# Attention layer, 16 images on one core: the first image's preparation reordered, the output weight summed in place and split during the first scores

## The chip, the cores and the metric

The kernel runs on one core of a Trainium2 chip. The metric is the device time of one execution in microseconds (us), and the median of several runs is compared. Engines are named as in the profile: PE is TensorE's matmul, PEld its weight load, DVE VectorE, ACT ScalarE, POOL GpSimd, SP SyncE, which issues most of the transfers.

## The reference, cut to what matters

```python
# x: (16, 512, 32, 32) float32, the weights are 512 x 512
h = group_norm(x, gamma, beta)          # 32 groups, eps 1e-6
q, k, v = conv1x1(h, wq, bq), conv1x1(h, wk, bk), conv1x1(h, wv, bv)
attn = einsum('bci,bcj->bij', qf, kf) * 512 ** -0.5
attn = softmax(attn, axis=2)
out = einsum('bcj,bij->bci', vf, attn)
return x + conv1x1(out, wo, bo)
```

## The kernel before

Each image is a matrix h of 512 channels by 1024 positions. The kernel folds the weights: the scores need only the product of wk and wq (called `wkq`), and the output needs only the product of wv and wo (`wov`), with the biases folded in as `t_bias` (from wk and bq) and `out_bias` (from wo, bv and bo). Both products are formed once. Every fp32 product is made of three matmuls, high by high, high by low and low by high, where "high" is a copy rounded by ACT (a CAST row) and "low" is what DVE subtracts to get the rest. A call of `product` is therefore three matmuls, on lines 315, 316 and 317.

**Preparation, once.** SP loads wo, wv, wk, wq and the first image. PE transposes wo (L326), which needs `ident` from POOL (L268). ACT and DVE split the transposed wo, POOL subtracts for wv (L272). PE forms `wov` (48 matmuls), then `wkq` (48 matmuls), and in between the bias sums (L346, L350, L352): matmuls of one column. `wov` is copied to SBUF, split, and stored in DRAM (`kept_v`). Then `wkq` is copied to SBUF, four differences are made of it (L809 to L814), and seven blocks are split into `w_split` (L543 on ACT, `wt_high`; L799 and L803 on DVE, `wt_split`), which SP stores as `kept_t`. The statistics of the first image come from `bn_piece` and `group_variance`; `normalise` (L527) applies them, `sum_h` (L737 to L745) makes four sums of the blocks, and `high_h` and `low_h` (L536, L752) split seven blocks.

**Each image.** `make_t` forms T in two halves r of seven products p (order `T_ORDER`), each six matmuls. `make_scores` forms 28 products of six matmuls in the order `S_ORDER`: four of p=7, then two pairs of q with p = 1, 6, 5, 3, 2, 4. ACT takes a snapshot of the bank after some products (L640, `s_snapped`), and the next product into that bank waits for it. DVE adds (L913, `add_s`), keeps the running maximum (L922, `max_step`), and takes the statistics of the next image from 8 pieces (L684), which SP loads. `make_v` forms 8 products of twelve matmuls; from the fifth on, j=4, it needs `v_split` (L938) to free a bank. `outputs_0` and `outputs_1` follow, 96 products. SP reloads `w_split` twice per image: from `kept_v` when T is done, from `kept_t` when V is done. The order on each engine is written out by hand, with semaphores between engines; an engine waits in order, so whatever stands behind a waiting instruction waits too.

Of the kernel before, what the change touches and what calls it, by code (L numbers as in the profile page):

```python
# [5 lines left out]
F32 = mybir.dt.float32  # L6
# [7 lines left out]
P = 128  # L14
# [17 lines left out]
T_AT = {p: n + 1 for n, p in enumerate(T_ORDER)}  # L32

# [20 lines left out]
def attention_program(nc, x, gamma, beta, wq, bq, wk, wv, bv, wo, bo, out):  # L54
# [15 lines left out]
    bq_d, *vec_d = [a.rearrange("(k p) -> p k", p=P) for a in (bq, gamma, beta, bo, bv)]  # L70
# [5 lines left out]
    with ExitStack() as ctx:  # L76
# [20 lines left out]
        bq_s, vecs = sb("bq_s", [KC]), sb("vecs", [4, KC])  # L97
        gamma_s, beta_s, bo_s, bv_s = (vecs[:, n, :] for n in range(4))
        t_bias, out_bias, t_step = sb("t_bias", [KC]), sb("out_bias", [KC]), sb("t_step", [2])
# [12 lines left out]
        for n, b_ in enumerate((S1, S3, S2, S4)):  # L112
            blocks[b_] = scores[:, 2 * n:2 * n + 2, :]

# [15 lines left out]
        wq_hi, wq_lo, wk_hi, wk_lo = big_hi[:, 0:4, :], big_lo[:, 0:4, :], big_hi[:, 4:8, :], big_lo[:, 4:8, :]  # L130
        wvs_hi, wvs_lo, wot_hi, wot_lo = big_hi[:, 8:12, :], big_lo[:, 8:12, :], big_hi[:, 12:16, :], big_lo[:, 12:16, :]
        wkq, wd_t, wov = scores[:, 0:4, :], scores[:, 4:8, :], scores[:, 12:16, :]
        first_v_hi, first_v_lo = (a[:, NJ:NJ + 6, :].rearrange("p (b k) n -> p b k n", k=2) for a in (big_hi, big_lo))
# [12 lines left out]
        bank = [ctx.enter_context(nc.psum_tensor(f"bank{n}", [P, 512], F32)) for n in range(8)]  # L146
# [4 lines left out]
        def o_bank(n):  # L151
            return bank[n]

        bq_in, vec_in = sem("bq_in"), sem("vec_in")
# [20 lines left out]
        wk_high, wq_high, wv_high, wot_high, wkq_copied, wov_copied, wt_high, wvs_high = (  # L175
            sem(n) for n in ("wk_high", "wq_high", "wv_high", "wot_high", "wkq_copied", "wov_copied", "wt_high",
# [7 lines left out]
        biases_set = sem("biases_set")  # L184
# [20 lines left out]
        def _(sp):  # L205
            for o in range(KC):
                sp.dma_start(wo_raw[:, o, :], w_d["o"][:, o, :]).then_inc(wo_in[o], 16)
            for o in range(KC):
                sp.dma_start(wv_raw[:, o, :], w_d["v"][:, o, :]).then_inc(wv_in[o], 16)
            for o in range(KC):  # L210
                sp.dma_start(wk_raw[:, o, :], w_d["k"][:, o, :]).then_inc(wk_in[o], 16)
                sp.dma_start(wq_raw[:, o, :], w_d["q"][:, o, :]).then_inc(wq_in[o], 16)
            for k in range(KC):
                sp.dma_start(full[:, k, :], x_d[0][:, k, :]).then_inc(x0_in[k], 16)

            sp.wait_ge(wvs_split, 3)
            sp.dma_start(kept_v[:, 0, :], big_hi[:, NJ:NJ + 6, :].rearrange("p a n -> p (a n)").bitcast(F32)).then_inc(kept_v_out, 16)
            sp.dma_start(kept_v[:, 1, :], big_lo[:, NJ:NJ + 6, :].rearrange("p a n -> p (a n)").bitcast(F32)).then_inc(kept_v_out, 16)
            sp.wait_ge(wt_split, 7)
            sp.dma_start(kept_t, w_split[:].bitcast(F32)).then_inc(kept_t_out, 16)  # L220
            sp.wait_ge(kept_v_out, 32)
            sp.wait_ge(kept_t_out, 16)

            def image(b, more):
# [8 lines left out]
                if more:  # L233
# [8 lines left out]
                sp.wait_ge(t_summed, count(b, 14, 14))  # L242
                sp.dma_start(w_split[:, :, 0:VW].bitcast(F32), kept_v).then_inc(wvs_in, 16)
                if more:
# [9 lines left out]
                    sp.wait_ge(v_summed, count(b, 8, 8))  # L254
                    sp.dma_start(w_split[:].bitcast(F32), kept_t).then_inc(wt_in, 16)


            images(sp, image)
# [4 lines left out]
        def _(pool):  # L263
            nc.gpsimd.memset(ident[:], 0.0).then_inc(consts_set, 1)
            nc.gpsimd.memset(minus_half[:], -0.5).then_inc(consts_set, 1)
            nc.gpsimd.memset(primer[:], 0.0).then_inc(consts_set, 1)
# [3 lines left out]
            for o in range(KC):  # L270
# [11 lines left out]

            deviation(0)
            prime()
# [28 lines left out]
        def _(pe):  # L313
# [8 lines left out]
            pe.wait_ge(consts_set, 4)  # L322
            for c in range(KC):
                pe.wait_ge(wo_in[c], 16)
                for n in range(KC):
                    mm = nc.tensor.transpose(bank[KC + n][:, cols(c)], wo_raw[:, c, cols(n)], ident[:])  # L326
                    if c == KC - 1:
                        mm.then_inc(wo_turned, 1)

            for o in range(KC):  # L330
                pe.wait_ge(wot_split, o + 1)
                pe.wait_ge(wv_split, o + 1)
                for c in range(KC):
                    mm = product(bank[c][:], wvs_hi[:, o, cols(c)], wvs_lo[:, o, cols(c)],
                                 wot_hi[:, o, :], wot_lo[:, o, :], o == 0, o == KC - 1)
                    if o == KC - 1:
                        mm.then_inc(wov_summed, 1)

            def bias_sums():

                pe.wait_ge(bq_in, 16)
                pe.wait_ge(vec_in, 16 * len(vec_d))
                pe.wait_ge(wov_copied, 1)
                for c in range(KC):
                    for o in range(KC):
                        nc.tensor.matmul(bank[0][:, c:c + 1], wk_raw[:, o, cols(c)], bq_s[:, o:o + 1],  # L346
                                         start=o == 0, stop=o == KC - 1, skip_group_check=True)
                for c in range(KC):
                    for o in range(KC):
                        nc.tensor.matmul(bank[0][:, KC + c:KC + c + 1], wot_hi[:, o, cols(c)].bitcast(F32),  # L350
                                         bv_s[:, o:o + 1], start=o == 0, stop=False, skip_group_check=True)
                        mm = nc.tensor.matmul(bank[0][:, KC + c:KC + c + 1], wot_lo[:, o, cols(c)].bitcast(F32),  # L352
                                              bv_s[:, o:o + 1], start=False, stop=o == KC - 1, skip_group_check=True)
                mm.then_inc(bias_summed, 1)

            for o in range(KC):
                pe.wait_ge(wk_split, o + 1)
                pe.wait_ge(wq_split, o + 1)
                for c in range(KC):
                    mm = product(bank[KC + c][:], wq_hi[:, o, cols(c)], wq_lo[:, o, cols(c)],  # L360
# [3 lines left out]
                if o == KC - 2:  # L364
                    bias_sums()
# [9 lines left out]
            def make_t(b):  # L375
                for r in range(2):
                    for p in T_ORDER:
                        if r == 0:
                            pe.wait_ge(h_split, count(b, 7, H_AT[OF_H[p]]))

                            pe.wait_ge(wt_split, T_AT[p])

                        if p == 4:
                            pe.wait_ge(o_scaled, count(b, 8, (1, 4)[r]))
                        if p == 7:
                            pe.wait_ge(o_scaled, count(b, 8, (2, 5)[r]))
                        if p == 5:
                            pe.wait_ge(o_scaled, count(b, 8, (3, 6)[r]))
# [675 lines left out]
```

## Time and profile before

| | us |
|---|---|
| median of 3 runs | 2062.42 (2057.86 to 2062.47) |
| profiled execution, its own time | 2057.07 |
| its span, first to last instruction | 2055.4 |
| PE busy | 2014.2 (98% of the span) |
| DVE busy | 1619.7 (79%) |
| ACT busy | 955.4 (46%) |

The difference between the profiled execution's time and its span is 1.7 us. A wait of PE lengthens the run directly, since PE is busy for nearly all of it outside the beginning.

### The profile page before, as it was taken

To read this page: it belongs to the slowest core of one execution; us is meant where nothing else is said; L and a number is where in the kernel's file an instruction comes from. 1 tells how busy PE (TensorE), PEld (TensorE's weight loads), DVE (VectorE), ACT (ScalarE), POOL (GpSimd) and SP (SyncE) were. 2 spreads that over 40 slices of the span, in tenths; PEclk is the share of its full clock that TensorE was granted. 3 is DMA by queue.
4 is the path that set the end of the run, shared out by engine and by line. 5 is a ranking of instruction groups with operands and counts; after the bars stand their busy time and mean duration, and the time that the engine had idled before them with its cause. 6 is when DMAs were issued, how large, how long until landed. Compare 5 with 4: busy or idle time off the path is not lost.

```text
span 2055.4 us, 26986 instructions
## 1 busy us (share of the span) xinstructions
PE 2014.2 (98%) x8848; PEld 1661.7 (81%) x8848; DVE 1619.7 (79%) x2112; ACT 955.4 (46%) x1427; POOL 325.2 (16%) x236
## 2 busy tenths in 40 slices
PE   7699999999999999999999999999999999999998
PEld 6488888888888888888888888888888888888886
DVE  3769697787978879697787978879697787968866
ACT  2635463452635445463453635445364443645442
POOL 1002012120201202012120202202011120201202
PEclk8799999999999999999999999999999999999999
DMA  3524335252343424335252343424335242343402
GB/s 123 222 96 143 113 153 143 85 139 108 125 135 153 101 83 146 109 153 143 86 138 112 122 133 153 106 77 150 105 153 143 98 127 112 127 128 153 93 10 41
DMA packets 57124, 248.79 MB, mean 121 GB/s; under 512 B 8208, under 2 KB 8208, under 8 KB 50192
## 3 DMA queue, kind: packets, MB, share of 16 engines
q1 hardware_dynamic: 36032, 214.97, 27.4%
q0 software_dynamic: 18432, 33.56, 10.9%
q10 hardware_dynamic: 2640, 0.01, 0.1%
q8 instruction: 10, 0.16, 0.0%
q14 instruction: 10, 0.08, 0.0%
HBM read 208.15 MB, written 73.92 MB: 137 GB/s over the span
## 4 chain that ended last, share of the span: by engine, by line
PE 91%; DMA 4%; DVE 2%; issue 1%; ACT 1%; POOL 0%; DVEq 0%; POOLq 0%; ACTq 0%
PE bank L315 30%; PE bank L317 30%; PE bank L316 30%; DMA out<-scores 4%; ACT scores L607 1%; DVE scores L835 0%; DVE h_lo L752 0%; DVE wide L954 0%; PE bank L352 0%; PE bank L350 0%; ACT room L527 0%; PE bank L346 0%; POOL out L307 0%; DVE w_split L803 0%; PE bank L326 0%
## 5 line engine op out<-in xcount | busy, mean ns | idle before, releaser
L315 PE MATMUL bank<-big_hi 128*128 128x512 f32 x1056 | 412.0, 390 | 0.8 <-DVE big_lo L760 0.8
L316 PE MATMUL bank<-big_lo,big_hi 128*128 128x512 f32 x1056 | 411.7, 390 | 0.0
L317 PE MATMUL bank<-big_hi,big_lo 128*128 128x512 f32 x1056 | 411.6, 390 | 0.0
L315 PE MATMUL bank<-big_hi,h_hi 128*128 128x512 f32 x896 | 349.8, 390 | 0.6
L317 PE MATMUL bank<-big_hi,h_lo 128*128 128x512 f32 x896 | 348.7, 389 | 0.0
L316 PE MATMUL bank<-big_lo,h_hi 128*128 128x512 f32 x896 | 348.7, 389 | 0.0
L913 DVE TENSOR_TENSOR scores<-bank,room 128x512 f32<-128x512 f32 x192 | 131.0, 689 | 194.2 <-ACT room L640 141.3
L640 ACT COPY room<-bank 128x512 f32<-128x512 f32 x192 | 112.8, 587 | 278.6 <-PE bank L317 278.6
L315 PEld LDWEIGHTS bank<-big_hi 128*128 128x128 f32 x1056 | 198.8, 188 | 42.6 <-DVE big_lo L760 1.2
L316 PEld LDWEIGHTS bank<-big_lo,big_hi 128*128 128x128 f32 x1056 | 198.8, 188 | 41.3
L317 PEld LDWEIGHTS bank<-big_hi,big_lo 128*128 128x128 f32 x1056 | 198.8, 188 | 41.2
L290 POOL PARTITION_ALL_REDUCE wide<-red x32 | 56.9, 1828 | 922.6 <-DVE red L922 922.6
L315 PEld LDWEIGHTS bank<-big_hi,h_hi 128*128 128x128 f32 x896 | 168.2, 188 | 40.1 <-issue 5.4
L315 PE MATMUL bank<-w_split,h_hi 128*128 128x512 f32 x512 | 199.2, 389 | 0.0
L316 PE MATMUL bank<-w_split,h_hi 128*128 128x512 f32 x512 | 199.2, 389 | 0.0
L317 PE MATMUL bank<-w_split,h_lo 128*128 128x512 f32 x512 | 199.2, 389 | 0.0
L315 PE MATMUL bank<-h_hi,w_split 128*128 128x512 f32 x448 | 177.5, 396 | 21.0 <-DVE w_split L803 8.3
L316 PEld LDWEIGHTS bank<-big_lo,h_hi 128*128 128x128 f32 x896 | 168.2, 188 | 34.8
L317 PEld LDWEIGHTS bank<-big_hi,h_lo 128*128 128x128 f32 x896 | 168.2, 188 | 34.8
L601 ACT CAST big_hi<-scores 128x512 fp32r<-128x512 f32 x256 | 147.8, 618 | 77.0 <-PE bank L317 75.0
L587 ACT CAST big_hi<-bank 128x512 fp32r<-128x512 f32 x128 | 75.2, 587 | 223.6 <-PE bank L317 223.5
L301 POOL PARTITION_ALL_REDUCE wide<-red x32 | 117.7, 3677 | 371.0 <-DVE red L950 357.1
(104 smaller groups left out, 3301.9 us busy)
## 6 DMA issues: line engine op xcount, KB each, us to landing
w_split<-kept_t SPq DMA_DIRECT2D x15, 3584.0 KB, 11.1
w_split<-kept_v SPq DMA_DIRECT2D x16, 3072.0 KB, 10.5
out<-scores POOLq DMA_DIRECT2D x128, 256.0 KB, 7.1
room<-in_x SPq DMA_DIRECT2D x30, 1024.0 KB, 5.9
room<-in_x SPq DMA_DIRECT2D x60, 256.0 KB, 3.6
red<-in_x SPq DMA_DIRECT2D x30, 256.0 KB, 3.4
wide<-in_x SPq DMA_DIRECT2D x30, 256.0 KB, 7.2
kept_t<-w_split SPq DMA_DIRECT2D x1, 3584.0 KB, 9.9
```

The lines of the kernel that those rows point to most:

```text
L290: nc.gpsimd.partition_all_reduce(wide[:, half, :], red[:, half, :], P, MAX_ALL).then_inc(max_all, 1)
L301: nc.gpsimd.partition_all_reduce(wide[:, half, :], red[:, half, :], P, ADD_ALL).then_inc(sum_all, 1)
L315: nc.tensor.matmul(o, a_hi, b_hi, start=start, stop=False, skip_group_check=True)
L316: nc.tensor.matmul(o, a_hi, b_lo, start=False, stop=False, skip_group_check=True)
L317: return nc.tensor.matmul(o, a_lo, b_hi, start=False, stop=stop, skip_group_check=True)
L587: nc.scalar.copy(v_hi[:, j, :], bank[v_ring[j % 4]][:]).then_inc(v_high, 1)
L601: nc.scalar.copy(p_hi[:, j, :], scores[:, half * NJ + j, :]).then_inc(p_high, 1)
L607: nc.scalar.activation(scaled(n), scaled(n), ACT.Identity, bias=out_bias[:, c:c + 1]).then_inc(o_done, 1)
L640: nc.scalar.copy(snap_s(q, n), bank[alpha_s[q % 2]][:]).then_inc(s_snapped, 1)
L913: nc.vector.tensor_tensor(scores[:, o, :], bank[at][:], snap_s(q, n), ALU.add).then_inc(s_added, 1)
```

## The change

It touches only the beginning and the first image; from the second image on the instructions are the same. SP now loads wk and wq first, then the first image (in the order of blocks 2, 3, 0, 1), then wv and wo. PE forms `wkq` first, into banks 0 to 3, then the rest of the bias sum of wk and bq, then the 16 transposes of wo, then `wov` into banks 4 to 7. The bias sum of wo and bv leaves PE: DVE makes it in the first scores with four multiply-and-reduce instructions (`tensor_tensor_reduce`), from wo and bv loaded again. `wkq` is no longer copied to SBUF, except one block (`b12_copy`). The copies of `wov`, its split and its store to `kept_v` move from the preparation into the first image: copies during T, the split on ACT (`high_wv`) and DVE (`first_weights`) during the first scores, written straight into `w_split`, so that the first V needs no reload. The first image's blocks are split partly inside its T. The pieces of the second image are loaded after `wvs_split`, and six of the eight are worked on at the end of the first pair of scores, the other two in the second pair. PE and SP have the first image written out ahead of their loop.

```diff
         def _(sp):
             for o in range(KC):
-                sp.dma_start(wo_raw[:, o, :], w_d["o"][:, o, :]).then_inc(wo_in[o], 16)
+                sp.dma_start(wk_raw[:, o, :], w_d["k"][:, o, :]).then_inc(wk_in[o], 16)
+                sp.dma_start(wq_raw[:, o, :], w_d["q"][:, o, :]).then_inc(wq_in[o], 16)
+            for k in (2, 3, 0, 1):
+                sp.dma_start(full[:, k, :], x_d[0][:, k, :]).then_inc(x0_in[k], 16)
             for o in range(KC):
                 sp.dma_start(wv_raw[:, o, :], w_d["v"][:, o, :]).then_inc(wv_in[o], 16)
...
+                if first:
+
+                    sp.wait_ge(t_split, 14)
+                    for c in range(KC):
+                        sp.dma_start(wo_again[c], w_d["o"][:, c, :]).then_inc(wo_back, 16)
+                    sp.dma_start(bv_rows, bv.partition_broadcast(P)).then_inc(bv_in, 16)
+                    sp.wait_ge(wvs_split, 3)
+                    for n in range(6):
+                        piece(n)
+                    sp.dma_start(kept_v, w_split[:, :, 0:VW].bitcast(F32)).then_inc(kept_v_out, 16)
...
+            bias_sum(0)
             for o in range(KC):
                 pe.wait_ge(wk_split, o + 1)
                 pe.wait_ge(wq_split, o + 1)
                 for c in range(KC):
-                    mm = product(bank[KC + c][:], wq_hi[:, o, cols(c)], wq_lo[:, o, cols(c)],
+                    mm = product(bank[c], wq_hi[:, o, cols(c)], wq_lo[:, o, cols(c)],
                                  wk_hi[:, o, :], wk_lo[:, o, :], o == 0, o == KC - 1)
...
+            for o in range(1, KC):
+                bias_sum(o)
+            pe.wait_ge(consts_set, 4)
+            for c in range(KC):
+                pe.wait_ge(wo_in[c], 16)
+
+            pe.wait_ge(t_bias_set, 1)
+            for n in range(KC):
+                for c in range(KC):
+                    mm = nc.tensor.transpose(bank[KC + n][:, cols(c)], wo_raw[:, c, cols(n)], ident[:])
+                mm.then_inc(wo_turned, 1)
+            pe.wait_ge(wot_split, KC)
...
+            act.wait_ge(wd_set, 4)
+            for p in W_ORDER:
+                high_wt(p)
+            for k in (2, 3):
                 normalise(0, k)
-            high_h(0, 0)
...
+            def high_wv(n):
+
+                act.wait_ge(t_summed, 14)
+                act.wait_ge(kept_t_out, 16)
+                if n == 2:
+                    act.wait_ge(wdv_set, 1)
+                else:
+                    act.wait_ge(wov_copied, KC)
+                nc.scalar.copy(wv_hi[:, n, :, :], wov_step if n == 2 else wov[n]).then_inc(wvs_high, 1)
...
                         nc.scalar.copy(scores[:, NJ + q, :], bank[alpha_s[q % 2]][:]).then_inc(c12_copied, 1)
+                    if first and pair == 0:
+                        high_wv(2)
...
+            def first_weights():
+
+
+                dve.wait_ge(t_split, 14)
+                dve.wait_ge(wov_copied, KC)
+                nc.vector.tensor_tensor(wov_step, wov[1], wov[0], ALU.subtract).then_inc(wdv_set, 1)
+                dve.wait_ge(wdv_set, 1)
+                for n in range(3):
+                    dve.wait_ge(wvs_high, n + 1)
+                    nc.vector.tensor_tensor(wv_lo[:, n, :, :], wov_step if n == 2 else wov[n],
+                                            wv_hi[:, n, :, :].bitcast(F32), ALU.subtract).then_inc(wvs_split, 1)
+                dve.wait_ge(wo_back, 16 * KC)
+                dve.wait_ge(bv_in, 16)
+                for c in range(KC):
+                    if c:
+                        dve.wait_ge(bv_used, c)
+                    nc.vector.tensor_tensor_reduce(out=wo_bv_terms, in0=wo_again[c], in1=bv_rows, scale=1.0,
+                                                   scalar=0.0, op0=ALU.mult, op1=ALU.add,
+                                                   accum_out=wo_bv[:, c:c + 1]).then_inc(bv_used, 1)
...
+                    if first and pair == 0:
+                        first_weights()
+                        for n in range(6):
+                            next_piece(b, n)
```

The order on SP's queue at the start, first before and then after (wk, wq, wo, wv are `in_wk` and so on, `room<-in_x` is the first image).

```order
L207 DMA scores<-in_wo 128x512 x4
L209 DMA scores<-in_wv 128x512 x4
L211 DMA scores<-in_wk 128x512
L212 DMA scores<-in_wq 128x512
L211 DMA scores<-in_wk 128x512
```

```order
L219 DMA scores<-in_wk 128x512
L220 DMA scores<-in_wq 128x512
L222 DMA room<-in_x 128x1024 x4
L224 DMA scores<-in_wv 128x512 x4
L226 DMA scores<-in_wo 128x512 x4
L229 DMA kept_t<-w_split 128x7168
```

The pair wk, wq stands four times on each side; it moved from the ninth place to the first, and the image moved ahead of wv and wo.

The order on ACT at the end of the first T and in the first scores (L640 and L696 are the snapshots, L644 and L703 the last copy of a pair, L606 is `high_wv`), before and then after.

```order
L583 CAST big_hi<-scores 128x512 x3
L640 COPY room<-bank 128x512 x6
L644 COPY scores<-bank 128x512 x2
L640 COPY room<-bank 128x512 x6
L644 COPY scores<-bank 128x512 x2
```

```order
L622 CAST big_hi<-scores 128x512 x3
L606 CAST w_split<-wide 128x1024
L606 CAST w_split<-room 128x1024
L696 COPY room<-psum 128x512 x6
L703 COPY scores<-psum 128x512 x2
L606 CAST w_split<-scores 128x1024
L696 COPY room<-psum 128x512 x6
L703 COPY scores<-psum 128x512 x2
```

The third cast of `high_wv` now stands between the copies of the first pair and the snapshots of the second.

The order on DVE in the first scores (L913 and L972 add, L922 and L981 take the maximum, L684 and L747 the statistics of a piece), before and then after.

```order
L684 BN_STATS bn<-wide 128x6 x2
L913 TENSOR_TENSOR scores<-bank,room 128x512 x2
L684 BN_STATS bn<-room 128x6 x2
L913 TENSOR_TENSOR scores<-bank,room 128x512 x2
L922 TENSOR_TENSOR red<-scores 128x1024
L913 TENSOR_TENSOR scores<-bank,room 128x512 x2
L922 TENSOR_TENSOR red<-red,scores 128x1024 x2
L913 TENSOR_TENSOR scores<-bank,room 128x512 x2
L696 BN_AGGR chan<-bn 128x2 x4
```

```order
L981 TENSOR_TENSOR red<-red,scores 128x1024 x2
L1026 TENSOR_TENSOR scores<-room,wide 128x1024
L1030 TENSOR_TENSOR w_split<-wide,w_split 128x1024
L1030 TENSOR_TENSOR w_split<-room,w_split 128x1024
L1030 TENSOR_TENSOR w_split<-scores,w_split 128x1024
L1037 ISA scores,wo_bv<-scores 128x512
L1037 ISA wo_bv 128x1
L1042 TENSOR_TENSOR out_bias<-wo_bv,vecs 128x4
L747 BN_STATS bn<-room 128x6 x2
L747 BN_STATS bn<-wide 128x6 x2
L972 TENSOR_TENSOR scores<-psum,room 128x512 x2
L747 BN_STATS bn<-room 128x6 x2
```

The two L1037 rows stand four times each. The work of `first_weights` and the six pieces now stands between the maxima of the first pair and the additions of the second, and the last two pieces stand ahead of the statistics' end (L759 after, L696 before).

## Rows read from the trace of the kernel before

**Rows 1.** The page: the span, and the busy time of each engine.
```profile
span 2055.4 us, 26986 instructions
PE 2014.2 (98%) x8848; PEld 1661.7 (81%) x8848; DVE 1619.7 (79%) x2112; ACT 955.4 (46%) x1427; POOL 325.2 (16%) x236
```

**Rows 2.** Windows, PE alone: width, PE busy, PE's granted clock, DMA share, GB/s.
```profile
0.00:4.00 4.00, 0.00 (x0) 1.00 0.36 69
0.00:8.00 8.00, 0.00 (x0) 1.00 0.72 190
0.00:16.00 16.00, 4.03 (x18) 1.00 0.90 282
0.00:20.00 20.00, 8.03 (x35) 1.00 0.93 307
...
84.00:98.00 14.00, 14.00 (x63) 1.00 0.34 114
```

**Rows 3.** Timeline of the start: start, us, engine, line, operation, tiles, idle before.
```profile
8.71 0.62 ACT L511 CAST big_hi<-scores 128x512 fp32r<-128x512 f32 x1 [6.06 <-DMA scores<-in_wv]
11.21 3.67 PE L326 MATMUL bank<-ident,scores 128*128 128x128 f32 x16 [11.21 <-POOL ident L268]
15.46 3.80 POOL L272 TENSOR_TENSOR big_lo<-scores,big_hi 128x512 fp32r<-128x512 f32 x3 [3.05 <-ACT big_hi L511]
23.95 4.83 DVE L684 BATCH_NORM_STATS2 bn<-room 128x6 f32<-128x512 f32 x8
31.61 0.16 DVE L722 SCALAR_TENSOR_TENSOR var_g<-square_g,chan_g 128x4 f32<-128x4 f32 x1
```

**Rows 4.** Windows, PE alone, where its granted clock falls and rises.
```profile
36.00:38.00 2.00, 2.00 (x20) 1.00 0.00 0
38.00:40.00 2.00, 2.00 (x17) 0.79 0.00 0
40.00:42.00 2.00, 2.00 (x11) 0.50 0.00 0
...
58.00:62.00 4.00, 0.00 (x0) 0.70 1.05 442
...
80.00:82.00 2.00, 1.38 (x3) 0.50 1.25 426
```

**Rows 5.** Timeline, 34 to 81 us, of PE, ACT and DVE.
```profile
34.83 3.63 PE L346 MATMUL bank<-bq_s,scores 128*128 128x1 f32 x32
51.44 1.99 ACT L550 CAST big_hi<-scores 128x1024 fp32r<-128x1024 f32 x2 [23.99 <-PE bank L352]
57.04 4.63 ACT L527 ACTIVATE room<-room,h_shift,h_scale 128x1024 f32<-128x1024 f32 x4
62.66 3.74 ACT L543 ACTIVATE w_split<-scores 128x512 fp32r<-128x512 f32 x7
65.73 2.49 DVE L803 TENSOR_TENSOR w_split<-scores,w_split 128x512 fp32r<-128x512 f32 x4
75.20 2.35 DVE L752 TENSOR_TENSOR h_lo<-scores,h_hi 128x1024 fp32r<-128x1024 f32 x2
80.62 0.79 PE L315 MATMUL bank<-h_hi,w_split 128*128 128x512 f32 x1 [3.43 <-ACT scores L574]
```

**Rows 6.** Timeline, the first scores and V, of PE, ACT and DVE.
```profile
98.46 0.39 PE L315 MATMUL bank<-big_hi,h_hi 128*128 128x512 f32 x1
121.14 2.49 DVE L922 TENSOR_TENSOR red<-red,scores 128x1024 f32<-128x1024 f32 x2
121.78 0.59 ACT L640 COPY room<-bank 128x512 f32<-128x512 f32 x1 [6.21 <-PE bank L317]
127.94 0.69 DVE L913 TENSOR_TENSOR scores<-bank,room 128x512 f32<-128x512 f32 x1 [4.31 <-ACT room L640]
138.52 2.48 DVE L922 TENSOR_TENSOR red<-red,scores 128x1024 f32<-128x1024 f32 x2
```

**Rows 7.** DMA issues: KB each, us from issue to landing.
```profile
kept_v<-big_lo SPq DMA_DIRECT2D x1, 1536.0 KB, 9.6
```

More of the change, by code:

```diff
@@ L210, in _, with image @@
             for o in range(KC):
[L211 to L218, printed above, removed]
+                sp.dma_start(wo_raw[:, o, :], w_d["o"][:, o, :]).then_inc(wo_in[o], 16)
             sp.wait_ge(wt_split, 7)
             sp.dma_start(kept_t, w_split[:].bitcast(F32)).then_inc(kept_t_out, 16)
-            sp.wait_ge(kept_v_out, 32)
-            sp.wait_ge(kept_t_out, 16)
-            def image(b, more):
+            def image(b, more, first=False):
                 sp.dma_start(out_d[b], x_d[b].rearrange("p k n -> k p n")).then_inc(rest_in, 16)
@@ L231, in piece @@
                                  x_d[b + 1][:, k, half * HALF:(half + 1) * HALF]).then_inc(piece_in[n % 6], 16)
-                if more:
+                if more and not first:
                     sp.wait_ge(h_split, count(b, 7, 7))
@@ L254, in image @@
                     sp.wait_ge(v_summed, count(b, 8, 8))
+                    if first:
+                        sp.wait_ge(kept_v_out, 16)
                     sp.dma_start(w_split[:].bitcast(F32), kept_t).then_inc(wt_in, 16)
-            images(sp, image)
+            image(0, True, True)
+            with sp.Fori(1, B - 1) as b:
+                image(b, True)
+            image(B - 1, False)
             for n in range(2 * KC):
@@ L499, in image @@
                     pe.wait_ge(wt_in, count(b, 16, 16))
-            images(pe, image)
+            image(0, True, True)
+            with pe.Fori(1, B - 1) as b:
+                image(b, True)
+            image(B - 1, False)
         @block.scalar
@@ L610, in image @@
             def image(b, more, first=False):
-                act.wait_ge(h_split, count(b, 7, 7))
+                if not first:
+                    act.wait_ge(h_split, count(b, 7, 7))
+                else:
+                    act.wait_ge(bias_summed, 1)
                 for r in range(2):
@@ L615, in image @@
                         snap(b, r, 0, "a", T_AT[4])
-                        if not first:
+                        if first:
+                            copy_wov(0)
+                            copy_wov(1)
+                        else:
                             for n in (KC, KC + 1):
@@ L624, in image @@
                     snap(b, r, 2, "y", T_AT[6])
+                    if r == 0 and first:
+                        high_h(0, 6, True)
                     high_t(b, r, "D1")
@@ L632, in image @@
                     high_t(b, r, "B21")
+                    if r == 0 and first:
+                        copy_wov(2)
+                        copy_wov(3)
+                if first:
+                    for n in range(2):
+                        high_wv(n)
                 for pair in range(2):
@@ L966, in image @@
                     q0, q1 = 2 * pair, 2 * pair + 1
-                    if more and pair == 0:
+                    if more and pair == 0 and not first:
                         for n in range(6):
                             next_piece(b, n)
-                    if more and pair == 1:
+                    if more and pair == 1 and not first:
                         dve.wait_ge(bn_set, count(b + 1, PIECES, PIECES))
@@ L973, in image @@
                     add_s(b, "C22", q1)
-                    if more and pair == 0:
+                    if more and pair == (1 if first else 0):
                         for n in range(6, 8):
                             next_piece(b, n)
+                    if first and pair == 1:
+                        dve.wait_ge(bn_set, count(b + 1, PIECES, PIECES))
                     if more and pair == 1:
```

288 lines of the change are left out of this document (147 added, 141 removed).

## The prediction

> **What bounds the kernel now.** The page first: PE is busy for 2014.2 of 2055.4 us [rows 1], so 41 us of idle are all that can be won by filling gaps; the other possible gain is PE work that is removed or that ran slowly. Then the windows of PE with its granted clock. From 84 to 98 us PE is busy throughout at clock 1.00 [rows 2], as it is in all later images. The beginning is different: PE starts at 11.21 us [rows 3], its clock falls to 0.50 between 38 and 42 us and stands there at 80 us [rows 4], and the first score matmul comes at 98.46 [rows 6]. Fourteen products of six matmuls lie ahead of it in T, and at full clock a product takes 1.36 us, a matmul 0.227: ACT begins the snapshot of the 17th score product at 121.78 [rows 6], and (121.6 - 98.46) / 17 is 1.36. So T alone is worth 84 x 0.227 = 19.1 us, and some 79 us of 98.5 are preparation.
>
> The timeline says where they go. 32 rows of one-column matmuls take 3.63 us at full clock [rows 5], and 64 more such rows, with the clock fallen, reach to 51.4, when ACT ends a wait of 23.99 us for them. Then ACT and DVE work nearly alone up to 80.62, where PE begins to run without a break [rows 5].
>
> **The start.** I take the loading from the mean rates: 0.28 MB in 4 us, 1.52 MB in 8, 4.51 in 16 and 6.14 in 20 [rows 2]. ACT saw the fifth transfer (1.31 MB in all, moved at about 7.4) at 8.71 [rows 3], so a transfer is seen 1.3 us after its last byte. In the new order: the first wk and wq are seen at 5.2 and 6.2, the fourth pair at 11.0, the image at 16.6, wv at 17.2 to 19.2, wo at 21.2 or so. A cast (0.62) and a subtraction (0.7) after 6.2 let PE begin on `wkq` at 7.7, instead of on transposes at 11.21.
>
> At what clock? The windows show 1.00 from the start [rows 2], but PE did nothing in them. When PE came back from a pause at 80.62 it was at 0.50 for 3 us [rows 4, 5], and I go by that: about 4.8 us at half clock, 11 of 48 matmuls, the rest at 0.227: 4.8 + 8.4 after 7.7 gives 21.0. The other bound is full clock at once, 2 us less. [...]
>
> **From `wkq` to T.** The remaining bias sum is 12 matmuls in 24 rows at 3.63/32: 2.7 us, to 23.7. ACT copies `t_bias` (0.3), then 16 transposes take 3.67 [rows 3], to 27.7. ACT and DVE split the last of four, 0.6 and 0.7, with DVE free: its statistics end 3.0 us after the last piece, as 31.77 stands to 28.78 [rows 3], thus 20.9, and four differences take 2.7 more. POOL's subtractions for wv, 3.80 for three [rows 3], now run from 22.0 to 25.8 behind the power for the statistics; in time. `wov` begins at 29.2. Its 48 matmuls take 10.9 at full clock, to 40.1.
>
> Here the clock matters once more. One-column matmuls and waits fill 21.0 to 24.0, and PE waits again after 27.7. Before, 4 us of such matmuls brought the clock down [rows 4, 5], and 3 us of pause did (0.70 in 58 to 62 [rows 4]). I take it to fall, which costs half of some 4.8 us: 2.4, so `wov` ends at 42.5. Bounds: 0 and 3.5.
>
> The other engines over the same time: ACT 3.74 for the high parts of `w_split` (28.4 to 32.2), 4.63 for normalising and 1.04 for the first block [rows 5], to 37.8; DVE's four of the seven low parts take 2.49, so 4.3 for seven, done by 34.4. Then sums and splits of 1.2 each [rows 5] on DVE: block 2 of seven at 41.4, 3 at 42.5, 4 at 43.7. These are ready when T wants them. The remaining three are not: ACT casts block 5 only after the snapshot of the third product, and DVE's queue holds sum and split of 1.2 each. The first half of T, 9.5 us of matmuls, takes 13.2 in my list (gaps of 1.7 ahead of the fifth and 1.9 ahead of the seventh product). The second half takes 9.6. T ends at 42.5 + 13.2 + 9.6 = 65.3, against 98.46: 33.2 us less.
>
> **What the first image gets instead.** I keep to the clock of the trace before; everything in it comes 33.2 earlier. `first_weights` waits for the maxima of the first pair, which end at 121.14 + 2.49 = 123.6 [rows 6]. The difference (1.2) ends at 124.9, and only then can ACT do the third cast of `high_wv` (1.04), to 126.0. Behind it on ACT stand the snapshots of the second pair; the first, at 121.78 before [rows 6], is now at 126.0 to 126.6. PE has (1, q=2) and (1, q=3) done at 123.1, and its next product waits for that snapshot: 3.5 us of new wait.
>
> DVE: three low parts, 1.2 each, to 128.4; four multiply-and-reduce with an accumulator read each, which no row shows. The nearest rows are 0.69 for 128x512 [rows 6] and 1.24 for twice the size; I take 0.95 with the read, 3.8 in all (bounds 2.8 and 6). Then six pieces, 4.83/8 each [rows 3], 3.6, which are loaded from 128.4 on. Total to 136.0. The next addition, at 127.94 before [rows 6], ends at 136.7. PE wants it for (4, q=2), at 134.0 before, now 137.5: just covered. Pieces 7 and 8 queue behind the store of `kept_v`, 3 MB, which took 9.6 us before [rows 7]; they are seen at about 141.5, and DVE waits for them ahead of all else. Then 1.2 for them, 3.0 of statistics, and 7.8 for four additions of 0.69 and four maxima of 1.24, with small gaps: the maxima end at 153.5 instead of 138.52 + 2.48 = 141.0 [rows 6]. The first `low_v` ends at 154.2. PE wants it for the fifth product of V, 38.1 + 10.9 us after 98.46, plus the 3.5: 151.0. That is 3.2 of wait. If the pieces came in time (138.3), `low_v` would be at 149.7 and the wait nothing.
>
> After that DVE is 9.9 late and PE 6.7; low parts of the second half are wanted at the very time that they are ready, so I add nothing. One return from half clock after these pauses costs about 1.6 (half of the 3.2 after 80.6 [rows 4]). Together: 3.5 + 3.2 + 1.6 = 8.3.
>
> **Sum.** -33.2 + 8.3 = -24.9, from the profiled execution's 2057.07: 2032. The three runs before lie 0.8 to 5.4 above that execution, so the median of after may lie above it too; I add 1 and say 2033.
>
> **Rivals.**
> A. The forecast: T some 33 us earlier, 5 to 11 given back. 2027 to 2037. Chance 0.55.
> B. The new waits are covered: the pieces land early, the clock stays up between `wkq` and `wov`. Gain 33.2 + 2.4 less 3.5 and a margin of 1: 31, 2026 and down to 2021. For it: DMA is mostly free there; against it: ACT's wait of 3.5 comes from order alone. Chance 0.17.
> C. More is lost in the first image: multiply-and-reduce at the upper bound (+2.2), and the lateness of DVE carries through the second half and into the next T (3 to 6), or the preparation's splits on ACT and DVE take 5 us longer. 2037 to 2050. DVE is busy 79% [rows 1], so such a delay ends within an image or two. Chance 0.21.
> D. The other side: PE stays at half clock. If the many short waits of the first T and scores kept the clock at 0.50 throughout, each matmul would take 0.43 instead of 0.227: over T, scores and V of the first image (84 + 168 + 96 matmuls) 348 x 0.2 = 70 us lost against 25 won. It decides from some 50 us at half clock, 120 matmuls or so over the 25 us. Against it: the clock came back within 4 us of unbroken work at 80.62 to 84 [rows 2, 4], and the gaps here are single ones between stretches of 5 to 20 us. Chance 0.03, with 0.04 for a net gain too small to be told (within 0.3%, 6 us, about what a measurement of this kernel can tell).
>
> **How the numbers follow.** A and B and C up to 2045 hold over 0.8: the range is 2022 to 2045. Faster by more than 0.3% (below 2056) holds A, B and C: 0.93; same 0.04; slower 0.03.
>
> **What would show it.** First score matmul at 65 (60 to 69) instead of 98.46. PE's first product near 7.7 and first at half clock. `wov` from 29 to 42. Two idle gaps of 1.5 to 2 us in the first half of T. A PE wait of about 3.5 us for ACT's snapshot some 25 us after the first score, and one of about 3 for `low_v` some 52 us after it. Later images unchanged. I would be wrong if the chain of waits showed ACT or DVE behind the block splits for longer, if transposes wait for wo, or if the written-out first image made PE wait for instructions.

## The result and the profile after

| | before | after |
|---|---|---|
| median of the runs, us | 2062.44 (2057.86 to 2063.1, 4) | 2036.33 (2035.51 to 2037.96, 4) |
| profiled execution, us | 2057.07 | 2037.96 |
| span, us | 2055.4 | 2036.3 |

The ratio is 0.988, 95% interval 0.9864 to 0.9896: faster by 1.2%. Forecast were 2033 us and the range 2022 to 2045. The medians are 26.1 us apart and the two profiled executions 19.1, because the median of before lies 5.4 above its profiled execution and that of after 1.6 below its own. All accounts below are of profiled executions.

The page of the kernel after, its first two rows, against [rows 1].

```profile
span 2036.3 us, 26714 instructions
PE 2005.2 (98%) x8784; PEld 1652.2 (81%) x8784; DVE 1624.8 (80%) x2119; ACT 954.0 (47%) x1425; POOL 325.5 (16%) x236
```

PE's share is 98% in both, so the page tells nothing of where 19 us went. Landmarks do: the first score matmul, and the reloads of `w_split`, which SP issues when V and T are done. The first score stood at 98.46 before [rows 6]. The two reloads of before, then the timeline rows of after:

```profile
158.49 0.35 SPq L255 DMA_DIRECT2D w_split<-kept_t  x1
...
221.05 0.58 SPq L243 DMA_DIRECT2D w_split<-kept_v  x1
```

```profile
6.95 0.76 PE L340 MATMUL psum<-big_hi 128*128 128x512 f32 x1 [0.43 <-DVE big_lo L827]
20.00 2.73 PE L352 MATMUL psum<-bq_s,scores 128*128 128x1 f32 x24
23.07 1.94 PE L375 MATMUL psum<-ident,scores 128*128 128x128 f32 x16 [0.34 <-ACT t_bias L575]
27.64 0.50 PE L340 MATMUL psum<-big_hi 128*128 128x512 f32 x1 [2.63 <-DVE big_lo L852]
63.04 0.39 PE L340 MATMUL psum<-big_hi,h_hi 128*128 128x512 f32 x1
...
135.52 0.34 SPq L275 DMA_DIRECT2D w_split<-kept_t  x1
...
201.95 0.62 SPq L261 DMA_DIRECT2D w_split<-kept_v  x1
```

So the lead over the kernel before is 98.46 - 63.04 = 35.4 us at the first score, 23.0 at the end of the first V, 19.1 at the end of the second image's T, and still 19.1 at the end. More was won in the preparation than the net shows, and 16.3 us were given back within the next 140 us.

Where it was given back is in the list of PE's waits up to 170 us (total, times, longest), of which these are three lines.

```profile
PE psum L340 <- ACT room L696: 3.5, 1, 3.5
PE psum L340 <- DVE big_lo L997: 3.2, 1, 3.2
PE psum L340 <- DVE h_lo L816: 3.1, 2, 1.6
```

The first two are the two waits of the forecast; the third is the two gaps in T. From 170 to 204 us one more, in the second image's T, where before there was none:

```profile
PE psum L340 <- DVE scores L885: 2.3, 1, 2.3
```

The timeline shows the chain behind the first two. DVE's difference of the output weight (L1026) releases ACT's cast (L606), behind which the snapshots stand; then DVE waits 6.62 us for the last two pieces, and the low part of v is that much later.

```profile
88.13 1.22 DVE L1026 TENSOR_TENSOR scores<-room,wide 128x1024 f32<-128x1024 f32 x1
89.46 1.04 ACT L606 CAST w_split<-scores 128x1024 fp32r<-128x1024 f32 x1 [9.31 <-DVE scores L1026]
90.41 1.07 ACT L696 COPY room<-psum 128x512 f32<-128x512 f32 x2
91.14 0.76 PE L340 MATMUL psum<-big_hi,h_hi 128*128 128x512 f32 x1 [3.45 <-ACT room L696]
109.28 1.33 DVE L747 BATCH_NORM_STATS2 bn<-room 128x6 f32<-128x512 f32 x2 [6.62 <-DMA room<-in_x]
121.68 0.79 PE L340 MATMUL psum<-w_split,h_hi 128*128 128x512 f32 x1 [3.23 <-DVE big_lo L997]
```

And windows of PE with its granted clock (columns as in [rows 2]) show what follows each pause.

```profile
80.00:90.00 10.00, 7.68 (x34) 0.99 0.00 0
90.00:95.00 5.00, 3.87 (x9) 0.50 0.19 66
95.00:100.00 5.00, 5.00 (x20) 0.84 0.93 274
120.00:125.00 5.00, 3.32 (x8) 0.55 0.93 372
125.00:130.00 5.00, 5.00 (x19) 0.76 0.11 39
```

A mean of 0.84 over 5 us is 1.6 us at 0.50; with the 5 us before and 0.2 at the end of the window of 0.99 that is 6.8 us at half clock, of which PE paused 1.3: 5.5 us of work that took twice its time, 2.7 us lost. The second spell is 4.5 + 2.4 us, less 1.2 of pause: 2.9 lost. The third, after the wait in the second image, is 3.4 us long (0.72 over 198 to 204): 1.7 lost. The account closes: 3.5 + 3.2 + 2.7 + 2.9 = 12.3 of the 12.4 us up to the end of V, and 2.3 + 1.7 = 4.0 of the 3.9 after it. ("Half clock" is 0.50 in the column: the matmuls from 92 to 96 us start 0.43 us apart, those around them 0.23.)

### The profile page after: what moved, and what is told of

The parts are those of the page before. It is cut to its first block, busy times and chain, and to the rows that moved or that the text cites. A ratio compares the mean times of both kernels' runs of the same rounds, so it can differ in the third digit from the quotient of the medians.

```text
span 2036.3 us, 26714 instructions
## 1 busy us (share of the span) xinstructions
PE 2005.2 (98%) x8784; PEld 1652.2 (81%) x8784; DVE 1624.8 (80%) x2119; ACT 954.0 (47%) x1425; POOL 325.5 (16%) x236
## 4 chain that ended last, share of the span: by engine, by line
PE 86%; DMA 5%; DVE 1%; issue 1%; ACT 1%; POOL 0%; DVEq 0%; POOLq 0%; ACTq 0%
PE psum L340 29%; PE psum L342 28%; PE psum L341 28%; DMA out<-scores 5%; ACT scores L646 1%; DVE scores L885 0%; DVE wide L1013 0%; DVE red L981 0%; POOL out L332 0%; DVE scores L1019 0%; DVE scores L1005 0%; DVE scores L972 0%; DVE scores L1007 0%; POOLq L79 0%; DVE big_lo L992 0%
## 5 line engine op out<-in xcount | busy, mean ns | idle before, releaser
L340 PE MATMUL psum<-big_hi 128*128 128x512 f32 x1056 | 413.2, 391 | 3.1 <-DVE big_lo L852 2.6
L341 PE MATMUL psum<-big_lo,big_hi 128*128 128x512 f32 x1056 | 412.6, 391 | 0.0
L342 PE MATMUL psum<-big_hi,big_lo 128*128 128x512 f32 x1056 | 412.6, 391 | 0.0
L340 PE MATMUL psum<-big_hi,h_hi 128*128 128x512 f32 x896 | 351.5, 392 | 4.0 <-ACT room L696 3.5
L341 PE MATMUL psum<-big_lo,h_hi 128*128 128x512 f32 x896 | 350.1, 391 | 0.0
L342 PE MATMUL psum<-big_hi,h_lo 128*128 128x512 f32 x896 | 350.0, 391 | 0.0
L972 DVE TENSOR_TENSOR scores<-psum,room 128x512 f32<-128x512 f32 x192 | 130.9, 689 | 195.2 <-ACT room L696 141.8
L696 ACT COPY room<-psum 128x512 f32<-128x512 f32 x192 | 112.7, 587 | 274.6 <-PE psum L342 274.6
L340 PEld LDWEIGHTS psum<-big_hi 128*128 128x128 f32 x1056 | 199.1, 189 | 44.5 <-DVE big_lo L852 2.9
L341 PEld LDWEIGHTS psum<-big_lo,big_hi 128*128 128x128 f32 x1056 | 199.3, 189 | 41.6
L340 PE MATMUL psum<-w_split,h_hi 128*128 128x512 f32 x512 | 200.7, 392 | 3.2 <-DVE big_lo L997 3.2
L342 PE MATMUL psum<-w_split,h_lo 128*128 128x512 f32 x512 | 200.4, 391 | 0.0
L341 PE MATMUL psum<-w_split,h_hi 128*128 128x512 f32 x512 | 200.4, 391 | 0.0
L640 ACT CAST big_hi<-scores 128x512 fp32r<-128x512 f32 x256 | 147.8, 619 | 75.2 <-PE psum L342 73.2
```

The source lines that it names most:

```text
L340: nc.tensor.matmul(o, a_hi, b_hi, start=start, stop=False, skip_group_check=True)
L341: nc.tensor.matmul(o, a_hi, b_lo, start=False, stop=False, skip_group_check=True)
L342: return nc.tensor.matmul(o, a_lo, b_hi, start=False, stop=stop, skip_group_check=True)
L640: nc.scalar.copy(p_hi[:, j, :], scores[:, half * NJ + j, :]).then_inc(p_high, 1)
L696: nc.scalar.copy(snap_s(q, n), bank[alpha_s[q % 2]][:]).then_inc(s_snapped, 1)
L972: nc.vector.tensor_tensor(scores[:, o, :], bank[at][:], snap_s(q, n), ALU.add).then_inc(s_added, 1)
```

## The experiments

All are timed against the kernel before on the same chip; "after" stands for the changed kernel. The landmark "first score" is the start of the first score matmul in each trace.

**The changed kernel again.**

> The changed kernel once more, to have it beside the next three. All theories: 2036 us (2035 to 2038), first scores begin some 35 us earlier than before, V of the first image ends some 23 us earlier, and PE waits 3.5 us for ACT's snapshot and 3.2 us for DVE's low part of v. If the 2.3 us wait of PE in the second image's T is an accident of the transfers, it differs here; if the new order makes it, it is here again.

Measured: 2037.58 us (2034.25 to 2040.85), ratio 0.9898 (0.9872 to 0.9924), 21.9 below the median of before in the same measurement. First score at 63.06, waits of 3.5 and 4.0, and 2.1 us in the second image's T. By the same windows the three spells at half clock cost some 1.7, 2.4 and 1.7 here, against 2.7, 2.9 and 1.7 in the first trace: the first wait is 3.5 us long in both, and what came behind it is not the same. The wait in the second image's T is made by the new order, not an accident: it also came in the next three kernels (1.2, 1.2, 2.2).

**The output weight's difference taken earlier on DVE (e1).**

```diff
                     q0, q1 = 2 * pair, 2 * pair + 1
...
+                    if first and pair == 0:
+                        dve.wait_ge(t_split, 14)
+                        dve.wait_ge(wov_copied, KC)
+                        nc.vector.tensor_tensor(wov_step, wov[1], wov[0], ALU.subtract).then_inc(wdv_set, 1)
                     add_s(b, "C22", q0)
```

> The difference of the output weight is taken on DVE ahead of the first scores' additions, where DVE stood idle for 8 us, so ACT's third cast no longer waits and the snapshots behind it are in time. Theory 1 (two waits in series on one DVE chain: the second one is set by DVE and by the late pieces): PE's 3.5 us wait for the snapshot goes, but DVE's chain is only 1.2 us shorter, so PE then waits some 8 us instead of 3.2 for the low part of v; the time falls by 1 to 2 us only, to 2035. Rival (the waits add up, each can be taken away by itself): 3.5 us and the half-clock spell after it, 2.8 us, are won, 2030.

Measured: 2035.29 us (2034.0 to 2036.98). PE's waits from 60 to 170 us:

```profile
PE psum L340 <- DVE big_lo L997: 3.3, 1, 3.3
PE psum L340 <- DVE scores L972: 3.2, 1, 3.2
```

The wait for ACT is gone and the time is the same within the noise, as theory 1 says; the rival's 2030 falls. The place was not quite as expected: part of the wait came back at the first addition of the second pair (L972), which DVE gives only after the six pieces. It was "just covered" in the forecast, and is the next wait in the line.

**The store behind the pieces (e2).**

```diff
                     for n in range(6):
                         piece(n)
-                    sp.dma_start(kept_v, w_split[:, :, 0:VW].bitcast(F32)).then_inc(kept_v_out, 16)
...
                         piece(n)
+                    if first:
+                        sp.dma_start(kept_v, w_split[:, :, 0:VW].bitcast(F32)).then_inc(kept_v_out, 16)
```

> The 3 MB store of the split output weight is issued behind the loads of the last two pieces instead of ahead of them. Theory 1 (the last two pieces stand behind the store, DVE waited 6.6 us for them, and PE in turn 3.2 us for DVE): DVE's wait for the pieces goes from 6.6 to under 1 us, PE's 3.2 us wait for v's low part and the half-clock spell after it (2.8 us) go, 6 us in all, 2030; the wait for the snapshot (3.5) stays. Rival (the pieces are late because they are issued late, whatever is ahead of them): DVE still waits 3 us or more, and the time stays within 1 us of 2036.

Measured: 2029.48 us (2026.95 to 2030.69). DVE's wait for the pieces in `room` fell from 6.6 to 0.4 us, and one wait of PE is left between 60 and 170 us:

```profile
PE psum L341 <- ACT room L697: 3.4, 1, 3.4
```

Theory 1 holds: the two pieces were late because 3 MB of store stood ahead of them in the queue. In after that store took 13.0 us to land:

```profile
kept_v<-w_split SPq DMA_DIRECT2D x1, 3072.0 KB, 13.0
```

The 9.6 us of [rows 7], with which the forecast reckoned, are for half as much, 1536 KB. It was the second of two such stores, issued at 56.31 and 56.68, so both together had landed 10.0 us after the first was issued.

**Both (e12).**

> Both edits. Theory 1: the snapshot is in time, the pieces are in time; DVE gives v's low part at about 113.8 us of the run and PE wants it at 112.1, so a wait of 1 to 2 us is left and no half-clock spell or a short one: 10 to 11 us less, 2026. Rival of e1 (waits simply add): 12.4 us less, 2024. Rival of e2: no more than e1 alone gives.

Measured: 2029.39 us (2028.13 to 2031.05), 3 us above theory 1 and no better than the store alone. PE's wait at L973, the first addition of the second pair, is 3.1 us long: with the snapshot in time PE simply arrives there sooner. The 1.7 us expected at the low part of v were put at the wrong place; DVE's six pieces and bias sum between the pairs are the limit. Part of the gain was also lost again behind it: the first V ended at 128.30 instead of 131.05 with the store alone, but PE's wait in the second image's T was 2.2 us long with a spell at half clock behind it (0.50 in 192 to 194 us), instead of 1.2 without one (1.00 from 190 to 204), and the second image's T ended at 194.60 against 195.07.

**The whole split in DVE's idle time (e4).**

```diff
+                    if first and pair == 0:
+                        first_weights()
                     add_s(b, "C22", q0)
                     add_s(b, "C22", q1)
+                    if first and pair == 0:
+                        for n in range(6):
+                            next_piece(b, n)
...
                     if first and pair == 0:
-                        first_weights()
-                        for n in range(6):
-                            next_piece(b, n)
+                        first_bias()
```

`first_bias` is the last part of `first_weights`, the sum with bv; ACT's third cast goes ahead of the first snapshot.

> The whole split of the output weight is done ahead of the first scores' additions, where DVE stood idle for 8 us (ACT's three casts ahead of the first snapshot), the six pieces are loaded and worked on in the first pair, and only the bias sum stays at its end. Theory 1 (all of what was given back comes from DVE's queue at the turn of the pairs and the spells at half clock behind its waits): no PE wait over 0.5 us in the first scores and V, no half-clock spell there, V of the first image ends at 123 to 124 us instead of 135.5, and DVE is not late in the second image; the time falls by 12 to 16 us, 2020 to 2025. Rival 1 (the same work on DVE moves the waits elsewhere: first snapshot, or the maxima): V ends at 127 or later, 2028 or more. Rival 2 (PE's wait of 1.2 to 2.3 us in the second image's T is one of the output stores, not of DVE's lateness): it stays here.

Measured: 2022.18 us (2020.96 to 2024.37), ratio to before 0.9828 (0.981 to 0.9847). From 60 to 170 us there is no PE wait in the list at all, and the clock is full throughout:

```profile
60.00:140.00 80.00, 80.00 (x354) 1.00 0.49 181
```

The first V ends at 123.4 instead of 135.5. Both rivals fall; the wait in the second image is gone too, so it was DVE's lateness that made it. How late DVE was shows at its last four output products of the first image, behind which its last stores come. Before and in after:

```profile
202.15 2.48 DVE L960 TENSOR_TENSOR scores<-bank,wide 128x512 f32<-128x512 f32 x4
180.75 2.48 DVE L1019 TENSOR_TENSOR scores<-psum,wide 128x512 f32<-128x512 f32 x4
```

That is 43.7 us behind the end of V before and 45.2 in after; here it is 43.7 again (167.09). In the traces where it is 44.7 to 46.3, PE waits 0.7 to 2.3 us at this place, and where it is 43.7, not at all or 0.6 (e7 below). DVE's own wait for the stores was there before, 2.5 us, is 5.6 in after and 3.4 here.

DVE's rows show where the work went: into the time in which it stood idle for 8.0 us in after.

```profile
68.42 1.23 DVE L1024 TENSOR_TENSOR scores<-room,wide 128x1024 f32<-128x1024 f32 x1
69.68 1.23 DVE L1028 TENSOR_TENSOR w_split<-wide,w_split 128x1024 fp32r<-128x1024 f32 x1
70.83 1.22 DVE L1028 TENSOR_TENSOR w_split<-room,w_split 128x1024 fp32r<-128x1024 f32 x1
71.96 1.22 DVE L1028 TENSOR_TENSOR w_split<-scores,w_split 128x1024 fp32r<-128x1024 f32 x1
76.52 0.69 DVE L970 TENSOR_TENSOR scores<-psum,room 128x512 f32<-128x512 f32 x1 [3.35 <-ACT room L696]
```

**Scale and shift behind the subtractions that PE waits for (e6).** `affine(0)` moves behind the loop over `wot_lo` on DVE.

> As e4_split_first, and the three small instructions of the first image's scale and shift are put behind the four subtractions for the transposed weight. In the changed kernel two of the three took 0.91 and 1.20 us instead of 0.15 while POOL subtracted for wv. Theory: they are lengthened by POOL's instructions, and stand ahead of what PE waits for; the output weight's product begins 1.2 us sooner, and the time is 1 to 1.5 us under e4. Rival: the subtractions themselves are lengthened by POOL in their place, and nothing is won.

Measured: 2018.16 us (2017.7 to 2021.58), ratio 0.981 (0.9791 to 0.983). First score 61.96, against 63.26 in the kernel without this edit, 1.3 us sooner, as expected. The median is 4.0 lower, more than the 1 to 1.5 of the theory, and the rest is not shown to come from the edit: T of the second image ends 1.3 us sooner (184.99 against 186.30), T of the sixth at the same time (678.06 against 678.07), though the instructions in between are the same. The rows of DVE in after, and then in this one:

```profile
22.85 0.91 DVE L790 TENSOR_TENSOR h_scale<-vecs,rstd 128x4 f32<-128x4 f32 x1
23.79 1.20 DVE L792 TENSOR_TENSOR mean_scaled<-chan_g,h_scale 128x4 f32<-128x4 f32 x1
25.11 2.48 DVE L852 TENSOR_TENSOR big_lo<-psum,big_hi 128x512 fp32r<-128x512 f32 x4
```

```profile
23.97 2.48 DVE L848 TENSOR_TENSOR big_lo<-psum,big_hi 128x512 fp32r<-128x512 f32 x4 [0.81 <-ACT big_hi L578]
26.38 0.15 DVE L788 TENSOR_TENSOR h_scale<-vecs,rstd 128x4 f32<-128x4 f32 x1
26.56 0.16 DVE L790 TENSOR_TENSOR mean_scaled<-chan_g,h_scale 128x4 f32<-128x4 f32 x1
```

POOL subtracts from 21.25 to 24.98 in after and from 21.60 to 25.33 here. The four subtractions that read PSUM take 2.48, whether POOL works in the first 1.4 us of them (here) or not (in after); the two small ones take 0.15 and 0.16 instead of 0.91 and 1.20 once POOL is done. The rival falls. Why the small ones are lengthened and the others are not, no run shows.

**One-column matmuls put back (a3).** 32 more of them, 64 rows, ahead of the transposes.

> The changed kernel with 32 more one-column matmuls (64 rows) ahead of the transposes, as many as the change took off PE; the output stays the same. Theory: they stand on the path, at full clock for some 4.5 us and at half clock after that, so the time rises by 9 to 13 us, to 2046 to 2049. Rival (the preparation is then bound by ACT, DVE and POOL, and PE has slack there): less than 4 us, under 2041.

Measured: 2047.66 us (2042.44 to 2048.19), first score 73.31, so 10.3 us later, as the theory said; the rival falls. The windows show the granted clock falling while they run:

```profile
20.00:24.00 4.00, 4.00 (x38) 1.00 0.06 20
24.00:28.00 4.00, 4.00 (x25) 0.62 0.00 0
28.00:32.00 4.00, 4.00 (x20) 0.50 0.00 0
```

**The bias sum of wo and bv taken out of the kernel before (b1)** (that term is left out of its output).

> The kernel before without the 32 matmuls of the bias sum of wo and bv; out_bias is bo alone, so that term is left out. Theory: 13 us of one-column matmuls at half clock, from 38.3 to 51.4, stood on the path, and the clock stays up: the first score matmul comes 13 to 14 us earlier, at about 85, and the time falls by as much, to 2046. This is then some 13 of the 35 us that the change wins ahead of the first scores. Rival (ACT and DVE bound that stretch through their splits of wkq and of the blocks): less than 8 us.

Measured: 2045.37 us (2043.6 to 2046.77), first score 87.48, 11.0 us earlier than in [rows 6]; the theory put 13 to 14 at that landmark and 2046 on the time. The rival, under 8, falls. The clock did not stay up, as the theory had it: the granted clock is 0.82 in 38 to 40 us and 0.66 in 40 to 44, at the end of the 32 rows that are left and behind them.

**The blocks of the first image split ahead of its T (u1).**

> The changed kernel with all seven blocks of the first image split ahead of its T, as before the change, instead of partly inside. Theory: T begins at about 46.7 us instead of 40.4 but runs without its two gaps (3.1 us), so the first scores begin some 3 us later, 2039 to 2040. Rival (the splits inside T cost as much in gaps as they save): within 1 us of 2037.

Measured: 2042.66 us (2041.05 to 2046.01), first score 69.08, 6.0 later, twice what the theory said. Of these some 2 us lie ahead of the edit's place: `wov` ended at 42.3 instead of 40.3 us, begun 0.9 later (PE waited 4.0 us for DVE behind the transposes, 2.6 in after) and with a longer spell at half clock (some 6.8 us, 3.4 in after). PE paused 6.1 us ahead of T, and T began at half clock (0.79 and 0.71 in the next two windows):

```profile
40.00:48.00 8.00, 2.45 (x11) 0.79 0.98 371
48.00:54.00 6.00, 5.47 (x18) 0.71 0.00 0
```

**The two products in a row with the splits, not beside them (u2).** `act.wait_ge(wov_summed, KC)` ahead of `high_wt`.

> The changed kernel, but ACT starts the split of w_split only when the output weight's product is done, as if PE's 11 us of it stood ahead of ACT's and DVE's work as before. Theory (a third of the win is that PE sums the output weight while ACT and DVE split): the split starts at 38.7 instead of 25.7, T some 11 us later, 2047 to 2049. Rival (PE's clock and the one-column matmuls account for the win, and the order of the two products is worth little): under 2042.

Measured: 2050.25 us (2046.65 to 2051.76), first score 77.49, 14.4 us later; the theory said some 11, and 2047 to 2049. The rival falls. PE waits 8.5 us at its longest, again with a spell at half clock behind it (0.50 from 48 to 58 us).

**The gaps in T (e7).** The fourth block sum ahead of T, the last three casts one place earlier.

> As e6_split_affine, with the fourth block sum ahead of the first T and the casts of the last three blocks each one place earlier on ACT, so that they don't stand behind a snapshot that waits for PE. Theory (the two gaps of 1.6 us in the first T come from this order alone): both go, 3 us less than e6_split_affine, 2015. Rival (DVE's splits bound that stretch): one gap stays, 1.5 us less or nothing.

Measured: 2017.59 us (2015.62 to 2020.99), ratio 0.98 (0.9787 to 0.9814), beside 2018.16 of the kernel without it: no difference that can be told. Both gaps are gone from PE's waits, but in the profiled execution the clock fell earlier, while the last one-column matmuls ran (1.00 in 21 to 22 us, 0.72 in 22 to 23), and the transposes took 3.65 us instead of 1.94; the first score came 0.9 us sooner. A wait of 0.6 us was back in the second image's T. Whether 3 us are to be had when the clock does not fall stays open.

```profile
20.00:24.00 4.00, 3.66 (x28) 0.80 0.04 15
24.00:28.00 4.00, 3.34 (x16) 0.50 0.02 4
28.00:32.00 4.00, 3.26 (x8) 0.50 0.00 0
```

## Why the prediction was right, and where it was off

**The gain ahead of the first scores** was forecast at 33.2 and measured at 35.4. The runs split it. Taking out the sum with bv gives 11.0 in the old order, and putting as many matmuls back costs 10.3 in the new. The overlap of the output weight's product with the splits is worth 14.4, the blocks inside T 6.0 by that run, or some 4 without what lay ahead of T. PE's first product begins at 6.95; before, its first work of all, the transposes, began at 11.21, 4.3 later, which is read from rows and not tested. The four are 35.7 with 11.0 and 6.0, near the whole, but each was taken by itself and they need not add up; that they come so near is partly chance.

Of the terms of the sum: `wkq` ended at 20.0 and not 21.0. The transposes took 1.94 and not 3.67, since the clock was still full (1.00 from 23 to 25 us), and ended at 25.0 and not 27.7. The wait for DVE behind them was 2.6 and not 1.5, so `wov` began at 27.6 instead of 29.2; DVE's two lengthened instructions (e6) stood ahead of what PE waited for. The clock did fall, as forecast, but for 3.4 us, not 4.8, and `wov` ended at 40.3 instead of 42.5. These 2.2 us are the whole difference between 33.2 and 35.4: from there to the first score it took 22.7 against 22.8, with gaps of 1.5 and 1.6 instead of 1.7 and 1.9.

The half clock at the very start was right. In windows of after that read 1.00, 5 and 6 matmuls fall into 2 us, then 10 (their starts are 0.43 us apart up to 10.93, and 0.23 from 11.34 on):

```profile
7.00:9.00 2.00, 2.00 (x5) 1.00 1.08 370
9.00:11.00 2.00, 2.00 (x6) 1.00 1.06 410
11.00:13.00 2.00, 2.00 (x10) 1.00 1.02 406
```

The clock column says nothing there; the number of matmuls does. That PE would begin so was an estimate, from its return at 80.62 alone. The 4.8 us and 11 matmuls put on it, and the 4.8 us taken again for `wov`, stand in none of the rows that the forecast cites (behind 80.62 it was 3 us); in after the start took 4.4 us and 10 matmuls, from 6.95 to 11.34, and the spell under `wov` 3.4 us.

**The two waits of the first image** were forecast at 3.5 and 3.2 and measured at 3.5 and 3.2 (4.0 in the second trace), at the places named. That ACT's queue makes the one (e1) and the store ahead of the last pieces the other (e2) is shown, as is that all of it hangs on the place of `first_weights` (e4). The first is right in every step: DVE's difference ends 26.3 us after the first score, against 26.4 in the forecast. The size of the second is luck in part, since two misses of 2.9 us cancel in it. Counted from the first score, PE wants the low part of v at 55.4, against 52.5 in the forecast, which left out the 2.7 us that PE loses at half clock behind the first wait. And it goes on at 58.6, against 55.7, because the last pieces are there at 46.2 and not 43.0: the store ahead of them took 13.0 us and not 9.6.

**The step that was mis-sized** is "One return from half clock after these pauses costs about 1.6". There were three returns, one after each wait, and they cost 2.7, 2.9 and 1.7, or 7.3 in place of 1.6; in the second trace 1.7, 2.4 and 1.7, or 5.8. So the count failed first: the forecast has two waits of over 3 us some 25 us apart, cites a pause of 3 us that brought the clock down, and still pays for one return. The 1.6 came from 80.62, where PE's clock came back about 3 us after it began. Behind 51.21 in the same trace it took some 4.9 us, and up to 5.7 in after.

**The step that failed** is "low parts of the second half are wanted at the very time that they are ready, so I add nothing". In the second half they were indeed in time, but DVE's lateness came out later: in the second image's T PE waits 2.3 us for an addition on DVE, which waited 5.6 us for stores of the first image's output; DVE had made the output products for them 1.6 us later than before, counted from the end of V. With DVE in time (e4) PE's wait is gone. Why the stores then take longer still (the addition comes 3.2 us later than before, of which 1.6 are DVE's) is not shown. PE lost 2.3 us there and 1.7 at half clock behind it, 4.0 in all, which is what rival C had for this (3 to 6).

**How near the number is, and how much of that is luck.** Together -35.4 + 16.3 gives -19.1, against -24.9 forecast. What was given back is 16.3 us, twice the 8.3 of the sum and above the 5 to 11 of rival A, in whose 2027 to 2037 the median falls. By mechanism the result is A with a part of C. Of the 8.0 us too much, 2.2 are made good by the preparation, which leaves the profiled execution off by 5.8. The median is off by 3.3 only, since 1 us was added for it and the profiled execution of after is the slowest of its four, 1.6 above their median.

Rivals B and D fall: neither wait was covered, the pieces came late and not early, the clock fell between `wkq` and `wov`, and it came back each time. The written-out first image made PE wait for no instructions that the waits show.

## What to carry to other kernels

When work is moved into a stage that runs at PE's pace, ask where each engine's queue is idle there, not only whether it has time in total: the split of the output weight and the six pieces cost 12 us at the turn of the two pairs and nothing 20 us earlier (e4, where the first V ended at 123.4 instead of 135.5). Count each wait of PE by itself, with the spell at half clock behind it: in after and its second trace the waits of 2.1 to 4.0 us were each followed by one that cost 1.7 to 2.9 us, half of the wait to nine tenths of it, while the waits of 1.2 us in e1 and e2 and the gaps of 1.5 and 1.6 us in T were followed by none. To take one of two waits in series away may win nothing until the other goes too (e1: 2035.29 us, against 2036.33 and 2037.58). And a large store belongs behind the small loads that somebody waits for (e2: DVE's wait for them fell from 6.6 to 0.4 us).

## What the runs showed of the hardware that was not expected

- Two DVE instructions on 128x4 elements took 0.91 and 1.20 us beside POOL's subtractions, 0.15 and 0.16 without.
- 16 transposes of 128x128 fp32 took 3.65 us in e7, where the granted clock is 0.50, and 1.94 at full clock in after. At the start of the kernel before they took 3.67, though the column reads 1.00 there.
- `tensor_tensor_reduce` on 128x512 showed as a row of 0.69 us and an accumulator read of 0.08; one every 0.73 us, where 0.95 had been taken.
- The clock falls at different moments in executions of the same preparation: the spell that ends under the output weight's product was 3.4 us long in after and 10.2 in e2, and the first score came at 63.04 and 64.44. It was 10.2 in e7 too. With single executions a few us apart (2034 to 2041 for the changed kernel), small edits of the beginning can't be told by their times.
